# Attention scores of one stage: keys laid out block-diagonally, two heads per matmul

## The chip, the cores and the metric

The kernel runs on one core of a Trainium2 chip. The core has a matmul engine (TensorE, PE in the rows), a vector engine (VectorE, DVE), a scalar engine (ScalarE, ACT), GpSimd (POOL) and SyncE (SP), which starts the transfers here. Each engine works through its own instructions in order and waits on semaphores for the others. The metric is the device time of one execution in microseconds (us). The kernel before takes 2413.01 us, the median of three runs (2412.48 to 2414.86).

## The reference

The program is four layers, each an attention followed by a feed-forward part, over 64 sequences of 64 tokens of width 128. The change lies in the second of the eight parts, the feed-forward of layer 0, which is itself an attention whose values come from experts:

```python
def _L0_ffn_ref(x, w_q, w_k, w_gate, value_experts, output_experts):
    # HEADS, DIM_HEAD, EXPERTS = 8, 64, 8; x is the layer-normed stream
    q = (x @ w_q).reshape(b, n, HEADS, DIM_HEAD).transpose(0, 2, 1, 3)
    k = (x @ w_k).reshape(b, n, HEADS, DIM_HEAD).transpose(0, 2, 1, 3)
    gates = jax.nn.sigmoid((x @ w_gate).reshape(b, n, HEADS, EXPERTS).transpose(0, 2, 1, 3))
    gm = jax.nn.one_hot(jnp.argmax(gates, axis=-1), EXPERTS, dtype=x.dtype) * gates
    values = jnp.einsum('bhne,ehdk,bnd->bhnk', gm, value_experts, x)
    sim = jnp.einsum('bhid,bhjd->bhij', q * DIM_HEAD ** (-0.5), k)
    sim = jnp.where(causal_mask, jnp.finfo(sim.dtype).min, sim)
    out = jnp.einsum('bhij,bhjk->bhik', jax.nn.softmax(sim, axis=-1), values)
    out = jnp.einsum('bhne,ehkd,bhnk->bhnd', gm, output_experts, out)
    return out.sum(axis=1)
```

## The kernel before

`l0_ffn` runs over 8 groups (g) of 4 tiles (t); a tile is 128 tokens, two sequences (b) of 64. The 8 heads go in 4 pairs (c), of two heads (a) each. The q and k projections put the two heads of a pair on partitions 0 to 63 and 64 to 127, so that qT and kT are [128, 4 pairs, 512 tokens].

Each engine has its program written out by hand, and the order of work is the order of the calls. For each tile PE does the 8 expert values (`expert_values`, L971), one matmul per expert, and DVE picks by a mask after each (`pick`, L1201 and L1206). Between them PE transposes the outputs of the tile before the last (`turn_out`, L1018) and the probabilities of the tile before (`turn_probs`, L997). Then come `scores` (L981 the causal mask, L987 the products) and `values` (L1010). DVE does the row maximum (L1215) and the subtraction (L1218) of the scores; ACT the exponential (L1111); DVE the sums, their reciprocals and a product with the gate (L1224, L1226, L1229), and later the scaling of the outputs (L1237). POOL multiplies the picked values by the gate (`gate_values`, L917).

At the end of a group PE also projects q and k of the next (`project`, L962), and ACT copies each projection out of PSUM (`copy_q`, L1094; `copy_k`, L1100), between its copies of the turned outputs (L1124), and then does the gate's tanh (L1104), for which DVE waits (L1191). Then PE runs 32 matmuls of the output experts (L1027), each for a product that DVE makes (L1247). A semaphore in `scores` makes PE wait until the scores of the tile before are subtracted (`sub_done`). POOL begins the stage with three fills or casts (`setup_done`), for which all wait, and then copies the first input (L905).

A kernel line that is one matmul of fp32 numbers shows as two MATMUL records: the 16 products of a tile are 32 records. The third stage, `l1_xattn`, has the layout that the change brings: L1470 is its mask, L1476 its score products, L1499 its value products, L1724 the row maximum, L1606 its key copies.

Of the kernel before, what the change touches and what calls it, by code (L numbers as in the profile page):

```python
# [15 lines left out]
ALU = mybir.AluOpType  # L16
ACT = mybir.ActivationFunctionType
AX = mybir.AxisListType

P = 128  # L20
SEQ = 64
# [3 lines left out]
G = 4  # L25
GROUPS = TILES // G
GT = G * P
# [51 lines left out]
def count(n):  # L79

    return n + 1


def after(eng, sem, value):

    if not isinstance(value, int) or value > 0:
        eng.wait_ge(sem, count(value))
# [18 lines left out]
class Core:  # L106
# [29 lines left out]
    def sb(self, ctx, name, shape, dt=F32):  # L136
        return ctx.enter_context(self.nc.sbuf_tensor(name, shape, dt))

    def ps(self, ctx, name, shape=(P, 512), dt=F32):
        return ctx.enter_context(self.nc.psum_tensor(name, list(shape), dt))  # L140

    def sem(self, name):
        return self.ctx.enter_context(self.nc.semaphore(name))
# [46 lines left out]
def bcast(ap, axis, n):  # L190

    ap = ap.unsqueeze(axis)
    shape = list(ap.shape)
    shape[axis] = n
    return ap.broadcast_to(shape)
# [41 lines left out]
def norm_gpsimd(core, nc, pool, s, u, m=G, eps=1e-5):  # L237

    pool.wait_ge(s.mv, count(u * m + m))
    pool.sem_inc(s.may_invert, 1)  # L240
    nc.gpsimd.tensor_scalar(core.ve[:, 0:m], core.mv[:, 0:m, 1], eps, None, ALU.add).then_inc(s.eps, 1)  # L241
    pool.wait_ge(s.eps, count(u + 1))
    nc.gpsimd.tensor_tensor(core.rs[:, 0:m], core.ve[:, 0:m], core.half[:, 0:m], ALU.pow).then_inc(s.rstd, 1)
# [567 lines left out]
def l0_ffn(core, nc, d):  # L811
# [10 lines left out]
    H, HD, E = 8, 64, 8  # L822
    C = H // 2
# [5 lines left out]
    with ExitStack() as ctx:  # L829
        sb = lambda name, shape, dt=F32: core.sb(ctx, "l0f_" + name, shape, dt)  # L830
        ps = lambda name, shape=(P, 512), dt=F32: core.ps(ctx, "l0f_" + name, shape, dt)
        sem = core.counters(1)
        causal = sb("causal", [P, SEQ], BF16)
# [9 lines left out]
        oh_bf = sb("oh_bf", [P, G, P], BF16)  # L843
        ohT = sb("ohT", [P, GT], BF16)
        qT = sb("qT", [P, C, GT])
        kT = sb("kT", [P, C, GT])
        val = sb("val", [P, 2, H, HD])
        v2 = sb("v2", [P, 2, 2, C, 2, HD])
        diff = sb("diff", [P, H, SEQ])
        prob = sb("prob", [P, 2, H, SEQ])  # L850
        mx = sb("mx", [P, 2, H])
# [4 lines left out]
        z = sb("z", [P, Z, GT])  # L856
        yT = core.xn[:, 0, :, :].rearrange("p j d -> p (j d)")
        work = [ps(f"work{i}") for i in range(2)]
        score = ps("score", (P, 1024)).rearrange("p (a n) -> p a n", a=2)
        turn, po, acc, misc = ps("turn"), ps("po"), ps("acc"), ps("misc")  # L860
        value_banks = (work[0], work[1], acc)
        oh_turn = misc[:, 256:512].bitcast(BF16)
# [1 line left out]
        setup_done, xs_ready, lg_done, chain = sem("setup_done"), sem("xs_ready"), sem("lg_done"), sem("chain")  # L864
        top_ready, tanh_done, oh_ready, oh_turned, ohT_ready = (sem("top_ready"), sem("tanh_done"), sem("oh_ready"),
                                                                sem("oh_turned"), sem("ohT_ready"))
        qk_done, qk_copied = sem("qk_done"), sem("qk_copied")
        ve_done, pick_done, v2_ready = sem("ve_done"), sem("pick_done"), sem("v2_ready")
        score_done, sub_done, exp_done, tot_done = sem("score_done"), sem("sub_done"), sem("exp_done"), sem("tot_done")
# [5 lines left out]
        gated, may_pick, max_done, sum_done = sem("gated"), sem("may_pick"), sem("max_done"), sem("sum_done")  # L875

        with nc.Block() as block:
# [19 lines left out]
            @block.gpsimd  # L897
            def _(pool):
                nc.gpsimd.tensor_copy(causal[:, :], core.const("caus_n")).then_inc(setup_done, 1)
                nc.gpsimd.memset(oh_bf[:, :, :], 0.0).then_inc(setup_done, 1)  # L900
                nc.gpsimd.memset(v2[:, :, :, :, :, :], 0.0).then_inc(setup_done, 1)

                def stage(u):
                    after(pool, ve_done, u * G * E)
                    nc.gpsimd.tensor_copy(xs[:, :], core.xnT[:, bass.ds(u * GT, GT)]).then_inc(xs_ready, 1)  # L905

                gate = top[:, 2, :].rearrange("p (t h) -> p t h", t=G)

                def gate_values(g, t):
                    n = g * G + t  # L910
                    pool.wait_ge(pick_done, count((n + 1) * E))
                    after(pool, pv_done, n - 1)
                    for b in range(2):
                        for a in range(2):
                            r = slice(b * SEQ, (b + 1) * SEQ)
                            after(pool, v2_ready, n * 4 + 2 * b + a)
                            nc.gpsimd.tensor_tensor(  # L917
                                v2[a * SEQ:(a + 1) * SEQ, t % 2, b, :, a, :],
                                val[r, t % 2, :, :].rearrange("p (c a) k -> p c a k", a=2)[:, :, a, :],
                                bcast(gate[r, t, :].rearrange("p (c a) -> p c a", a=2)[:, :, a], 2, HD),  # L920
                                ALU.mult).then_inc(v2_ready, 1)
                    pool.wait_ge(v2_ready, count(n * 4 + 4))

                def group(g, more):
                    for t in range(1, G):
                        if t == G - 1 and more:
                            stage(g + 1)
                        gate_values(g, t)
                    if more:
                        gate_values(g + 1, 0)  # L930
                    norm_gpsimd(core, nc, pool, ns, g)

                stage(0)
                gate_values(0, 0)
                group(0, True)
                with pool.Fori(1, GROUPS - 1) as g:
                    group(g, True)
                group(GROUPS - 1, False)

            @block.tensor  # L940
            def _(pe):
                pe.wait_ge(core.w_loaded[1], 16)
                pe.wait_ge(setup_done, count(3))

                def logits(u):
                    pe.wait_ge(xs_ready, count(u + 1))
# [29 lines left out]
                            later()  # L976

                def scores(g, t):
                    after(pe, sub_done, g * G + t)
                    for a in range(2):  # L980
                        nc.tensor.matmul(score[:, a, 0:C * SEQ], core.ident_bf[:, :], bcast(causal[:, :], 1, C),  # L981
                                         start=True, stop=False, skip_group_check=True)
                    for c in range(C):
                        for b in range(2):
                            for a in range(2):
                                r, tok = slice(a * HD, (a + 1) * HD), slice(t * P + b * SEQ, t * P + (b + 1) * SEQ)
                                ins = nc.tensor.matmul(score[b * SEQ:(b + 1) * SEQ, a, c * SEQ:(c + 1) * SEQ],  # L987
                                                       qT[r, c, tok], kT[r, c, tok], start=False, stop=True,
                                                       skip_group_check=True)
                    ins.then_inc(score_done, 1)  # L990

                def turn_probs(g, t):
# [92 lines left out]

            @block.scalar
            def _(act):
                act.wait_ge(setup_done, count(3))

                def copy_q(u, chunks):  # L1090
                    after(act, score_done, u * G)
# [4 lines left out]
                def copy_k(u, chunks):  # L1096
                    after(act, score_done, u * G)
                    for c in chunks:
                        act.wait_ge(qk_done, count(u * 2 * C + C + c + 1))
                        nc.scalar.activation(kT[:, c, :], work[c % 2][:, :], ACT.Copy).then_inc(qk_copied, 1)  # L1100

                def gate_tanh(u):
                    act.wait_ge(top_ready, count(u + 1))
# [66 lines left out]

            @block.vector
            def _(dve):
                dve.wait_ge(setup_done, count(3))
                prio = bcast(core.const("prio"), 1, G * H)
                gate = top[:, 2, :].rearrange("p (t h) -> p t h", t=G)

# [32 lines left out]

                def softmax(g, t):  # L1210
                    n = g * G + t
                    s = score[:, :, 0:C * SEQ].rearrange("p a (c k) -> p a c k", c=C)
                    by_pair = mx[:, t % 2, :].rearrange("p (c a) -> p a c", a=2)
                    dve.wait_ge(score_done, count(n + 1))
                    nc.vector.tensor_reduce(by_pair, s, AX.X, ALU.max).then_inc(max_done, 1)  # L1215
                    dve.wait_ge(max_done, count(n + 1))
                    after(dve, exp_done, n)
                    nc.vector.tensor_tensor(diff[:, :, :].rearrange("p (c a) k -> p a c k", a=2), s, bcast(by_pair, 3, SEQ),  # L1218
                                            ALU.subtract).then_inc(sub_done, 1)

                def totals(g, t):
                    n = g * G + t
# [1841 lines left out]
def program(nc, d, out):  # L3064
    with ExitStack() as ctx:
        core = Core(nc, ctx)
        l0_xattn(core, nc, d)
        l0_ffn(core, nc, d)
        late_weights(core, nc, d)
        l1_xattn(core, nc, d)  # L3070
        with ExitStack() as late:
            km = core.sb(late, "keys_by_head", [P, G, 2, 16, SEQ])
            l1_ffn(core, nc, km)
            narrow_attention(core, nc, d, 4, True, km)
            l2_ffn(core, nc, d)
            narrow_attention(core, nc, d, 6, False, km)
        l3_ffn(core, nc, out)
# [112 lines left out]
```

## Time and profile before

| what | value |
|---|---|
| median of the runs | 2413.01 us |
| the profiled execution's own time | 2412.48 us |
| its span, first to last instruction | 2410.3 us |
| PE busy in the span | 2090.6 us, 87% |
| DVE busy | 1657.9 us, 69% |
| ACT busy | 862.7 us, 36% |
| POOL busy | 610.8 us, 25% |
| mean granted TensorE clock | 0.922 of full |

The stage of the change runs from about 149 us to 850 us of the span. Busy shares are over the whole program; what decides is which engine waits for which in this stage. In the rows of a timeline the bracket at the end is the idle time of the engine just before the row, and what ended it; a row without a bracket followed its predecessor.

### The profile page before, as it was taken

To read this page: it belongs to the slowest core of one execution; us is meant where nothing else is said; L and a number is where in the kernel's file an instruction comes from. 1 tells how busy PE (TensorE), PEld (TensorE's weight loads), DVE (VectorE), ACT (ScalarE), POOL (GpSimd) and SP (SyncE) were. 2 spreads that over 40 slices of the span, in tenths; PEclk is the share of its full clock that TensorE was granted. 3 is DMA by queue.
4 is the path that set the end of the run, shared out by engine and by line. 5 is a ranking of instruction groups with operands and counts; after the bars stand their busy time and mean duration, and the time that the engine had idled before them with its cause. 6 is when DMAs were issued, how large, how long until landed. Compare 5 with 4: busy or idle time off the path is not lost. (4 is left out here: it accounts for less than half of the span.)

```text
span 2410.3 us, 39647 instructions
## 1 busy us (share of the span) xinstructions
PE 2090.6 (87%) x12969; PEld 1154.9 (48%) x12971; DVE 1657.9 (69%) x3378; ACT 862.7 (36%) x1527; POOL 610.8 (25%) x832
## 2 busy tenths in 40 slices
PE   4769899899999879999999899689979999769965
PEld 2634444444444446666666544245544444335531
DVE  4767676777777756777777589667746667446668
ACT  4511201201211046666666554223332222223435
POOL 4641110111111044455555333222200000111201
PEclk8579999999999989999999999789979999989976
DMA  4403212230320421111111000000003433210001
GB/s 103 148 1 71 55 44 45 53 71 17 71 53 18 105 82 35 34 33 35 31 34 35 24 1 1 1 12 12 11 20 93 109 82 82 63 21 12 12 3 35
DMA packets 131760, 106.43 MB, mean 44 GB/s; under 512 B 95400, under 2 KB 113704, under 8 KB 127152
## 3 DMA queue, kind: packets, MB, share of 16 engines
q1 hardware_dynamic: 131632, 104.84, 17.7%
q8 instruction: 66, 1.08, 0.2%
q14 instruction: 62, 0.51, 0.1%
HBM read 80.85 MB, written 2.97 MB: 35 GB/s over the span
## 5 line engine op out<-in xcount | busy, mean ns | idle before, releaser
L1027 PE MATMUL l0f_acc<-l0f_z,w_all 128*128 128x512 f32 x512 | 230.1, 612 | 21.3 <-DVE l0f_z L1247 21.3
L917 POOL TENSOR_TENSOR l0f_v<-l0f_val,l0f_top 64x256 f32<-64x256 f32 x128 | 78.3, 612 | 506.5 <-DVE l0f_val L1206 498.9
L971 PE MATMUL l0f_work<-w_all,l0f_xs 128*128 128x512 f32 x384 | 187.6, 612 | 11.5 <-DVE l0f_val L1201 10.8
L1027 PEld LDWEIGHTS l0f_acc<-l0f_z,w_all 128*128 128x128 f32 x512 | 99.6, 196 | 151.4 <-issue 125.4
L241 POOL TENSOR_SCALAR var_eps<-mean_var 128x4 f32<-128x4 f32 (+1 forms) x64 | 14.5, 227 | 544.7 <-DVE mean_var L225 542.8
L2285 PE MATMUL a_score<-keys_by_head,a_qT 128*64 128x512 f32 x512 | 144.3, 646 | 9.0 <-DMA keys_by_head<-w_all 9.0
L1206 DVE COPY_PREDICATED l0f_val<-l0f_oh,l0f_work 128x512 f32<-128x512 int32 x160 | 116.8, 730 | 46.8 <-PE l0f_work L971 28.8
L2777 DVE TENSOR_TENSOR l2f_hu<-l2f_act_g,l2f_pu 128x512 f32<-128x512 f32 x104 | 71.1, 684 | 69.2 <-ACT l2f_act_g L2703 68.0
L2652 PE MATMUL l2f_acc<-l2f_hid,w_all 128*128 128x512 f32 x208 | 107.4, 598 | 9.8 <-DVE l2f_hid L2783 9.8
L2703 ACT ACTIVATE l2f_act_g<-l2f_pg 128x512 f32<-128x512 f32 x104 | 61.5, 594 | 149.5 <-PE l2f_pu L2644 137.6
L1707 DVE TENSOR_REDUCE l1x_ms_k<-l1x_sq_k 128x8 f32<-128x512 f32 x64 | 43.9, 685 | 102.9 <-ACT l1x_sq_k L1593 102.9
L971 PEld LDWEIGHTS l0f_work<-w_all,l0f_xs 128*128 128x128 f32 x384 | 68.9, 192 | 86.5 <-issue 54.1
L2643 PE MATMUL l2f_pg<-xnT_all,w_all 128*128 128x512 f32 x208 | 109.0, 606 | 0.0
L2644 PE MATMUL l2f_pu<-xnT_all,w_all 128*128 128x512 f32 x208 | 108.0, 601 | 0.0
L1247 DVE TENSOR_TENSOR l0f_z<-l0f_oT,l0f_first_mask 128x512 f32<-128x512 f32 x128 | 87.3, 692 | 27.6 <-PE l0f_acc L1027 24.1
L1386 POOL TENSOR_TENSOR l1x_rs_q<-l1x_ms_q,minus_half 128x8 f32<-128x8 f32 x64 | 104.8, 1637 | 5.7 <-POOL l1x_ms_q L1382 0.8
L1395 POOL TENSOR_TENSOR l1x_rs_k<-l1x_ms_k,minus_half 128x8 f32<-128x8 f32 x64 | 104.7, 1636 | 5.4 <-POOL l1x_ms_k L1391 0.2
L1606 ACT ACTIVATE l1x_kb<-l1x_turn,cols 64x512 f32<-64x512 f32 x128 | 87.3, 682 | 51.3 <-PE l1x_turn L1459 50.5
L1247 DVE TENSOR_TENSOR l0f_z<-l0f_oT,w_all 128x512 f32<-128x512 f32 x128 | 88.7, 693 | 21.1 <-PE l0f_acc L1027 20.8
L2466 DVE TENSOR_REDUCE a_mx<-a_score 128x16 f32<-128x1024 f32 x64 | 78.0, 1219 | 32.9 <-PE a_score L2285 32.7
L2407 ACT ACTIVATE a_oT<-a_po 128x128 f32<-128x128 f32 x64 | 17.7, 277 | 210.4 <-PE a_po L2315 210.4
L1157 ACT ACTIVATE xn<-l0f_acc 128x512 f32<-128x512 f32 x8 | 4.8, 597 | 245.7 <-PE l0f_acc L1027 245.7
(362 smaller groups left out, 4804.5 us busy)
## 6 DMA issues: line engine op xcount, KB each, us to landing
l0f_first_mask<-onehots SPq DMA_DIRECT2D x32, 512.0 KB, 5.7
w_all<-onehots SPq DMA_DIRECT2D x32, 512.0 KB, 11.9
l1x_v<-l1x_vr SPq DMA_DIRECT2D x256, 64.0 KB, 2.1
w_all<-combination SPq DMA_DIRECT2D x40, 256.0 KB, 5.3
w_all<-in_weights SPq DMA_DIRECT2D x1, 4640.0 KB, 17.3
l0x_m_b<-running_max SPq DMA_DIRECT2D x16, 256.0 KB, 4.5
keys_by_head<-w_all SPq DMA_DIRECT2D x256, 8.0 KB
keys_by_head<-ctxT_all SPq DMA_DIRECT2D x256, 8.0 KB
```

The lines of the kernel that those rows point to most:

```text
L917: nc.gpsimd.tensor_tensor(v2[a * SEQ:(a + 1) * SEQ, t % 2, b, :, a, :], val[r, t % 2, :, :].rearrange("p (c a) k -> p c a k", a=2)[:, :, a ...
L971: nc.tensor.matmul(value_banks[e % 3][:, :], xs[:, t * P:(t + 1) * P], ve[:, e, :], start=True, stop=True).then_inc(ve_done, 1)
L1027: nc.tensor.matmul(acc[:, :], oe[:, n % E, n // E, :], z[:, n % Z, :], start=(n == 0), stop=(n == C * E - 1)).then_inc(acc_done, 1)
L1206: nc.vector.copy_predicated(val[:, t % 2, :, :], m_e, w3).then_inc(pick_done, 1)
L1247: nc.vector.tensor_tensor(z[:, n % Z, :], oT[:, n // E, :], masks[n // E][:, n % E, :], ALU.mult)\
L1386: nc.gpsimd.tensor_tensor(rs_q[:, :], ms_q[:, 1, :], core.half[:, 0:HU], ALU.pow).then_inc(rs_q_done, 1)
L1395: nc.gpsimd.tensor_tensor(rs_k[:, :], ms_k[:, 1, :], core.half[:, 0:HU], ALU.pow).then_inc(rs_k_done, 1)
L1606: ins = nc.scalar.activation(kb[r, :, :, a, :], turn1[r, :].rearrange("p (c b k) -> p c b k", c=C, b=2), ACT.Copy, scale=core.col("l1_kw") ...
L2285: ins = nc.tensor.matmul(s[b * SEQ:(b + 1) * SEQ, cols], qT[:, half, t * P + b * SEQ:t * P + (b + 1) * SEQ], km[:, t, b, bank * C:(bank + ...
L2643: nc.tensor.matmul(pg[n % 3][:, :], wg[:, c * P:(c + 1) * P], x_of(g), start=True, stop=True)
L2644: nc.tensor.matmul(pu[n % 3][:, :], wu[:, c * P:(c + 1) * P], x_of(g), start=True, stop=True)\
L2652: nc.tensor.matmul(acc[:, :], wd[:, c * P:(c + 1) * P], hid[:, n % 3, :], start=(c == 0), stop=(c == CH - 1)).then_inc(acc_done, 1)
```

## The change

The two-bank score tensor becomes two tensors of one bank, taken in turn by even and odd tiles, and `scores` waits for the subtraction of the tile before the last. The transposed keys are kept as `kb`, zero outside the blocks: for a tile, a sequence and a pair it is [128 partitions, 2 heads x 64 keys], with head 0's keys on the first 64 partitions and head 1's on the last 64. One matmul with all 128 partitions then gives the scores of both heads. It takes 16 KB per partition, where kT took 8. POOL fills it with zeros once, ahead of v2; ACT copies each key projection in two halves of 64 partitions. The maximum and the subtraction read the heads in their order.

```diff
-        kT = sb("kT", [P, C, GT])
+        kb = sb("kb", [P, G, 2, C, 2, SEQ])
-        score = ps("score", (P, 1024)).rearrange("p (a n) -> p a n", a=2)
+        score = [ps(f"score{i}") for i in range(2)]
...
+                nc.gpsimd.memset(kb[:, :, :, :, :, :], 0.0).then_inc(setup_done, 1)
                 nc.gpsimd.memset(v2[:, :, :, :, :, :], 0.0).then_inc(setup_done, 1)
...
-                pe.wait_ge(setup_done, count(3))
+                pe.wait_ge(setup_done, count(4))
...
                 def scores(g, t):
-                    after(pe, sub_done, g * G + t)
-                    for a in range(2):
-                        nc.tensor.matmul(score[:, a, 0:C * SEQ], core.ident_bf[:, :], bcast(causal[:, :], 1, C),
-                                         start=True, stop=False, skip_group_check=True)
+                    after(pe, sub_done, g * G + t - 1)
+                    nc.tensor.matmul(score[t % 2][:, :], core.ident_bf[:, :], bcast(causal[:, :], 1, H),
+                                     start=True, stop=False, skip_group_check=True)
                     for c in range(C):
                         for b in range(2):
-                            for a in range(2):
-                                r, tok = slice(a * HD, (a + 1) * HD), slice(t * P + b * SEQ, t * P + (b + 1) * SEQ)
-                                ins = nc.tensor.matmul(score[b * SEQ:(b + 1) * SEQ, a, c * SEQ:(c + 1) * SEQ],
-                                                       qT[r, c, tok], kT[r, c, tok], start=False, stop=True,
-                                                       skip_group_check=True)
+                            ins = nc.tensor.matmul(score[t % 2][b * SEQ:(b + 1) * SEQ, c * P:(c + 1) * P],
+                                                   qT[:, c, t * P + b * SEQ:t * P + (b + 1) * SEQ],
+                                                   kb[:, t, b, c, :, :].rearrange("p a k -> p (a k)"),
+                                                   start=False, stop=True, skip_group_check=True)
...
                         act.wait_ge(qk_done, count(u * 2 * C + C + c + 1))
-                        nc.scalar.activation(kT[:, c, :], work[c % 2][:, :], ACT.Copy).then_inc(qk_copied, 1)
+                        for a in range(2):
+                            r = slice(a * HD, (a + 1) * HD)
+                            ins = nc.scalar.activation(kb[r, :, :, c, a, :],
+                                                       work[c % 2][r, :].rearrange("p (t b k) -> p t b k", t=G, b=2),
+                                                       ACT.Copy)
+                        ins.then_inc(qk_copied, 1)
...
-                    nc.vector.tensor_reduce(by_pair, s, AX.X, ALU.max).then_inc(max_done, 1)
+                    nc.vector.tensor_reduce(mx[:, t % 2, :], s, AX.X, ALU.max).then_inc(max_done, 1)
```

PE in the first group, around the scores of the second tile, before (the number in front of a shape's first x is the output's partitions):

```order
L971 MATMUL l0f_work<-w_all,l0f_xs 128x512 x2
L981 MATMUL l0f_score<-l0f_causal,ident_bf 128x256 x2
L987 MATMUL l0f_score<-l0f_kT,l0f_qT 64x64 x16
L1010 MATMUL l0f_po<-l0f_v,l0f_probT 64x128 x8
L1038 MATMUL l0f_misc<-ident_bf,l0f_oh_bf 128x128 x4
```

and the same place after the change:

```order
L972 MATMUL l0f_work<-w_all,l0f_xs 128x512 x2
L981 MATMUL l0f_score<-l0f_causal,ident_bf 128x512
L985 MATMUL l0f_score<-l0f_kb,l0f_qT 64x128 x8
L1009 MATMUL l0f_po<-l0f_v,l0f_probT 64x128 x8
L1037 MATMUL l0f_misc<-ident_bf,l0f_oh_bf 128x128 x4
```

Nothing changes place; one mask matmul stands for two, and 8 products of 128 columns for 16 of 64.

ACT at the end of the first group, from the last two q copies to the copy after the output experts, before:

```order
L1094 ACTIVATE l0f_qT<-l0f_work 128x512 x2
L1118 ACTIVATE l0f_probT<-l0f_turn 128x512
L1100 ACTIVATE l0f_kT<-l0f_work 128x512 x3
L1124 ACTIVATE l0f_oT<-l0f_turn 128x4x128
L1100 ACTIVATE l0f_kT<-l0f_work 128x512
L1104 ACTIVATE l0f_top<-l0f_top 128x32
L1157 ACTIVATE xn<-l0f_acc 128x512
```

and after:

```order
L1093 ACTIVATE l0f_qT<-l0f_work 128x512 x2
L1122 ACTIVATE l0f_probT<-l0f_turn 128x512
L1101 ACTIVATE l0f_kb<-l0f_work 64x8x64 x6
L1128 ACTIVATE l0f_oT<-l0f_turn 128x4x128
L1101 ACTIVATE l0f_kb<-l0f_work 64x8x64 x2
L1108 ACTIVATE l0f_top<-l0f_top 128x32
L1161 ACTIVATE xn<-l0f_acc 128x512
```

Each key copy is two instructions now; they stand ahead of the copy of the turned outputs and of the tanh, as the single ones did.

## Rows read from the trace of the kernel before

**Rows 1.** timeline, second group, second tile: start, duration, engine, line, wait.
```profile
261.36 0.38 PE L981 MATMUL l0f_score<-l0f_causal,ident_bf 128*128 128x256 bf16 x2
...
261.67 0.69 PE L987 MATMUL l0f_score<-l0f_kT,l0f_qT 64*64 64x64 f32 x32
...
262.30 1.09 PE L1010 MATMUL l0f_po<-l0f_v,l0f_probT 128*64 128x128 f32 x16
262.44 0.69 DVE L1215 TENSOR_REDUCE l0f_mx<-l0f_score 128x8 f32<-128x512 f32 x1
262.78 2.68 POOL L917 TENSOR_TENSOR l0f_v<-l0f_val,l0f_top 64x256 f32<-64x256 f32 x4 [6.00 <-DVE l0f_val L1206]
...
264.81 0.17 DVE L1229 TENSOR_TENSOR l0f_tot<-l0f_tot,l0f_top 128x8 f32<-128x8 f32 x1
...
268.40 0.66 PE L1018 MATMUL l0f_turn<-consts,l0f_og 128*128 128x128 f32 x4 [2.04 <-DVE l0f_og L1237]
```

**Rows 2.** timeline, third stage, whose scores have the other layout.
```profile
1001.69 0.38 PE L1470 MATMUL l1x_score<-l1x_mask,ident_bf 128*128 x1
...
1002.00 1.09 PE L1476 MATMUL l1x_score<-l1x_kb,l1x_qT 128*64 128x128 f32 x16
...
1002.93 1.04 PE L1499 MATMUL l1x_po<-l1x_v,l1x_probT 128*64 128x128 f32 x16
...
1003.14 0.69 DVE L1724 TENSOR_REDUCE l1x_mx<-l1x_score 128x8 f32<-128x512 f32 x1 [0.21 <-PE l1x_score L1476]
```

**Rows 3.** timeline, line L1229 in later and earlier tiles.
```profile
182.14 0.57 DVE L1229 TENSOR_TENSOR l0f_tot<-l0f_tot,l0f_top 128x8 f32<-128x8 f32 x1
...
276.56 2.68 POOL L917 TENSOR_TENSOR l0f_v<-l0f_val,l0f_top 64x256 f32<-64x256 f32 x4 [11.11 <-DVE l0f_val L1206]
...
278.66 0.60 DVE L1229 TENSOR_TENSOR l0f_tot<-l0f_tot,l0f_top 128x8 f32<-128x8 f32 x1
...
805.78 0.56 DVE L1229 TENSOR_TENSOR l0f_tot<-l0f_tot,l0f_top 128x8 f32<-128x8 f32 x1
```

**Rows 4.** timeline, start of the stage.
```profile
149.95 1.80 POOL L901 MEMSET l0f_v<- 128x2048 f32 x1
...
152.45 1.94 PE L950 MATMUL l0f_misc<-w_all,l0f_xs 128*128 128x64 f32 x8 [4.05 <-POOL l0f_xs L905]
...
160.05 0.60 ACT L1100 ACTIVATE l0f_kT<-l0f_work 128x512 f32<-128x512 f32 x1 [0.26 <-PE l0f_work L962]
...
163.47 1.98 PE L971 MATMUL l0f_work<-w_all,l0f_xs 128*128 128x512 f32 x4 [0.69 <-ACT l0f_kT L1100]
```

**Rows 5.** lines by form, a larger fill: shape, count, busy us, mean ns.
```profile
L1859 POOL MEMSET keys_by_head<- 128x8192 f32 x1 | 6.9, 6923 | 0.1
```

**Rows 6.** timeline, third stage, two copies of 64 partitions.
```profile
999.57 1.38 ACT L1606 ACTIVATE l1x_kb<-l1x_turn,cols 64x512 f32<-64x512 f32 x2
```

**Rows 7.** timeline, end of the second group.
```profile
289.49 1.94 PE L962 MATMUL l0f_work<-xnT_all,w_all 128*128 x4
...
291.26 0.60 PE L1018 MATMUL l0f_turn<-consts,l0f_og 128*128 128x128 f32 x4
...
296.86 0.69 DVE L1237 TENSOR_TENSOR l0f_og<-l0f_po,l0f_tot 128x512 f32<-128x512 f32 x1 [4.74 <-PE l0f_po L1010]
...
297.85 0.60 ACT L1100 ACTIVATE l0f_kT<-l0f_work 128x512 f32<-128x512 f32 x1 [1.48 <-PE l0f_work L962]
...
298.35 0.59 ACT L1124 ACTIVATE l0f_oT<-l0f_turn 128x512 f32<-128x512 f32 x1
...
299.66 0.22 ACT L1104 ACTIVATE l0f_top<-l0f_top 128x32 f32<-128x32 f32 x1
...
300.84 0.17 DVE L1191 TENSOR_SCALAR l0f_top<-l0f_top 128x32 f32<-128x32 f32 x1
```

**Rows 8.** windows: us, busy by engine (records), granted clock, DMA share, GB/s.
```profile
268.40:272.70 4.30, 4.30 (x12) 2.37 (x13) 1.71 (x3) 0.60 (x1) 0.00 (x0) 0.60 1.06 236
356.00:360.30 4.30, 4.29 (x16) 2.41 (x17) 2.50 (x4) 1.19 (x2) 0.00 (x0) 1.00 1.01 211
```

More of the change, by code:

```diff
@@ L1087, in _ @@
             def _(act):
-                act.wait_ge(setup_done, count(3))
+                act.wait_ge(setup_done, count(4))
                 def copy_q(u, chunks):
@@ L1172, in _ @@
             def _(dve):
-                dve.wait_ge(setup_done, count(3))
+                dve.wait_ge(setup_done, count(4))
                 prio = bcast(core.const("prio"), 1, G * H)
@@ L1211, in softmax @@
                     n = g * G + t
-                    s = score[:, :, 0:C * SEQ].rearrange("p a (c k) -> p a c k", c=C)
-                    by_pair = mx[:, t % 2, :].rearrange("p (c a) -> p a c", a=2)
+                    s = score[t % 2][:, :].rearrange("p (h k) -> p h k", h=H)
                     dve.wait_ge(score_done, count(n + 1))
-                    nc.vector.tensor_reduce(by_pair, s, AX.X, ALU.max).then_inc(max_done, 1)
+                    nc.vector.tensor_reduce(mx[:, t % 2, :], s, AX.X, ALU.max).then_inc(max_done, 1)
                     dve.wait_ge(max_done, count(n + 1))
                     after(dve, exp_done, n)
-                    nc.vector.tensor_tensor(diff[:, :, :].rearrange("p (c a) k -> p a c k", a=2), s, bcast(by_pair, 3, SEQ),
-                                            ALU.subtract).then_inc(sub_done, 1)
+                    nc.vector.tensor_tensor(diff[:, :, :], s, bcast(mx[:, t % 2, :], 2, SEQ), ALU.subtract)\
+                        .then_inc(sub_done, 1)
                 def totals(g, t):
```

## The prediction

> **What bounds the kernel now.** I read the timeline of the stage first, then its waits, then the granted clock. In a tile DVE and PE take turns. [rows 1] show it for the second tile of the second group: PE's score products start at 261.67 and end at 262.36, DVE takes the row maximum (L1215) 0.08 us later, and with no wait in the row. From there DVE leads: maximum, subtraction, sums, gate product L1229, two picks, scaled outputs, and PE has idled 2.04 us when L1018 starts on those outputs at 268.40. Then PE leads to the next scores. So the end of the scores and DVE's chain behind it are on the path, and PE's time between scores and L1018 is not. At the end of a group PE leads alone: [rows 7] have L962 from 289.49 and L1018 at 291.26 without a wait, and DVE idles 4.74 us for PE's values before L1237. DVE then has its expert picking, ended by L1191, which waits for ACT's tanh (L1104).
>
> **The score products.** Before: 32 records of 64 rows by 64 columns, from 261.67 to the start of L1010 at 262.30, 0.63 us. After: 16 records of 128 rows and 128 columns. That form stands in the third stage [rows 2]: from L1476 at 1002.00 to L1499 at 1002.93 is 0.93 us, and from L1476 to DVE's maximum, which waits for it, is 1.14 us. In [rows 1] this last distance is 262.44 - 261.67 = 0.77. So the halves of the array that worked side by side on the two heads now work on one product whose other half is zeros: PE pays 0.93 - 0.63 = 0.30 us a tile, DVE starts 1.14 - 0.77 = 0.37 us later. The mask costs nothing either way: L981 to L987 is 0.31 us [rows 1], L1470 to L1476 0.31 us [rows 2].
>
> The Trainium skill (TensorEngine Tiling (Array Packing), Theoretical Speedup) gives up to 2x for a contraction of 64 or less, so taking the row tiles away should double the products. The rows of the two forms, 0.63 and 0.93 us, show a factor of 1.5. By the page the products would take 1.26 us, 0.63 more, and my term for the seven group ends below would be 4.4 us in place of 2.1; I go by the rows.
>
> The wait on the subtraction gains nothing. On DVE the subtraction of a tile stands ahead of all 8 picks of the next, and PE's scores stand behind the expert values that those picks release; no row of L981 has a wait on DVE [rows 1]. The second score bank removes a wait that is never last.
>
> What the delay of a tile becomes depends on its place:
> - *First tile of a group* (8): in seven, DVE first adds the outputs to x and takes statistics, and PE is ahead. 0. The very first tile has no such cover: at most 0.37, I take 0.1.
> - *Second tile, groups 2 to 7* (6): L1229 starts at 264.81 in 0.17 us, just ahead of the last of POOL's four products, which end at 262.78 + 2.68 = 265.46 [rows 1]. In 12 other places L1229 takes 0.52 to 0.60 us, of which [rows 3] have the first, one between and the last; the one at 278.66 ends at 279.26, and POOL's four products end at 276.56 + 2.68 = 279.24. So L1229 waits for a POOL product that has begun. Moved by 0.37 to 265.18 it falls into the last one and ends at 265.46 or so in place of 264.98: 0.48 x 6 = 2.9 us.
> - *Third tile of all, second tile of groups 1 and 8, fourth of group 8* (11): there L1229 already waits for POOL. Ready 0.37 later (279.03 in [rows 3]) it still ends with POOL at 279.24, since POOL's start hangs on the last pick and not on the scores. 0; without that shelter 11 x 0.37 = 4.1.
> - *Fourth tile, groups 1 to 7* (7): PE leads without a gap, so its own 0.30 counts: 2.1 us. No cover here.
>
> **The fill.** A POOL fill of 2048 elements takes 1.80 us [rows 4], one of 8192 takes 6.92 [rows 5]: 0.833 ns an element, so 4096 take 1.80 + 2048 x 0.000833 = 3.5 us. It stands ahead of the copy L905, and PE's first matmul L950 has idled 4.05 us for that copy [rows 4], DVE and ACT wait for PE. Nothing else runs there: +3.5, once; I see no way to hide it.
>
> **The key copies.** One copy of 128 partitions is 0.60 us [rows 4]. Two of 64 partitions in the third stage take 1.38 us for the pair [rows 6], one behind the other; they carry a scale for each partition, ours none. I take 0.61 apiece; the ends are 0.50 (the distance from a key copy at 297.85 to the next copy at 298.35 [rows 7]) and 0.69.
> - *Start of the stage*: 8 half copies from 160.05 end at 164.93, and the expert values L971, which started at 163.47 after a wait for the last key copy [rows 4], start at 164.98: +1.5 (ends 0.5 and 2.2).
> - *Group ends* [rows 7]: the third key copy starts at 297.85, its halves end at 299.07, L1124 follows, the fourth key's halves run from 299.57 to 300.79 and the tanh ends at 301.01. L1191 had started at 300.84: it starts 0.2 later, seven times, +1.4. Before, the tanh was done at 299.88, so the first 0.96 us of the longer copies are hidden behind DVE's expert picking. With 0.50 apiece all is hidden (0), with 0.69 it is 0.54 x 7 = 3.8.
> - Reading one bank instead of two changes nothing: the maximum takes 0.69 us in both forms [rows 1, 2].
>
> **Sum.** 3.5 + 1.5 + 0.1 + 2.9 + 2.1 + 1.4 = 11.5 us. The profiled execution took 2412.48 us by its own time, 0.5 under the median of the runs, so 2424.0 us. All lower ends together (no cost in the second tiles) give 3.5 + 0.5 + 2.1 = 6.1; all upper ends 3.5 + 2.2 + 0.4 + 2.9 + 4.1 + 2.1 + 3.8 = 19.0.
>
> **The clock** is the part that I can't place. [rows 8] have two stretches of the same work in two groups: at a mean granted clock of 0.60 PE gets through 12 records, at 1.00 through 16. The first is mostly at 1.2 GHz, and loses 4.30 x (1 - 0.60) = 1.7 us. Such stretches stand eight times in the stage, in four of the groups' third tiles and at four of their ends, and otherwise equal groups differ by them. A group that gets 1 us longer meets them elsewhere: I allow three more or fewer, 5 us.
>
> **Rivals.**
> - *No shelter at L1229*: what makes L1229 long could be something else than POOL's products, and the 11 delays come through: 2424.0 + 4.1 = 2428.1. For it: at 264.81 it runs in 0.17 amid them. Against: the ends match to 0.02 us [rows 3]. The Trainium skill (SBUF — State Buffer, SBUF: two separate sides) has VectorE with two SBUF inputs and GpSimd exclude each other for a whole instruction, which would give the shelter; these rows agree.
> - *Dear half copies*: 0.69 apiece adds 0.7 at the start and 2.4 at the group ends: 2427.1. For it the pair in [rows 6], against it the missing scale.
> - *Cheap products*: if a record costs the same 0.02 us (0.63 / 32) whatever its shape, 16 take 0.31 and PE gains 0.3 a tile: 3.5 + 1.5 + 1.4 - 2.1 = 4.3, 2416.8 us, which is no measurable change. Against it stands L1476 in [rows 2].
> - *The clock pays it back*, on the other side: if low stretches go, each gives 1.7 us. Four fewer leave 4.7 us, below what can be told from none; seven fewer cancel all, and all eight give 2410.4 us. For it: half of such places have none now. Against: PE's idle before L1018 stays about as long, so their cause stays.
>
> **Chances.** The forecast 0.67, no shelter 0.10, dear copies 0.08, cheap products 0.06, the clock 0.09. The first three are slower by over 0.2% (4.8 us, about what a measurement of this kernel can tell from no change): 0.85. Cheap products and two thirds of the clock case are within: 0.12; faster 0.03. The forecast's own range is 2419 to 2429, with the rivals 2416.5 to 2431.
>
> **What the new profile would show.** A 128x4096 fill of 3.5 us and PE's first matmul of the stage 3.5 us later; 16 score records and 0.93 us from the first to the values; DVE's maximum now with a wait on PE's scores; L1229 long in the second tiles too, with POOL's end; PE's idle before the turned outputs about as before; half copies of 0.60, and L1191 waiting for the tanh. The forecast is wrong if the maximum starts as early as before, if the halves overlap, or if the number of stretches below full clock moves by more than three.

## The result and the profile after

The changed kernel takes 2437.46 us in the median (2432.83 to 2439.78, six runs) against 2413.94; the ratio is 1.009, with a 95% interval of 1.0074 to 1.0107. Slower was forecast, with 2424.0 us and a range to 2431. The forecast size was half of the measured one, and the time lies outside the range.

The profiled execution took 2432.44 us, 20.0 more than that of before. Its timeline in the second group, second tile, against [rows 1]:

```profile
269.51 1.09 PE L985 MATMUL l0f_score<-l0f_kb,l0f_qT 128*64 128x128 f32 x16
270.43 1.04 PE L1009 MATMUL l0f_po<-l0f_v,l0f_probT 128*64 128x128 f32 x16
...
270.65 0.69 DVE L1218 TENSOR_REDUCE l0f_mx<-l0f_score 128x8 f32<-128x512 f32 x1 [0.30 <-PE l0f_score L985]
...
273.02 0.30 DVE L1232 TENSOR_TENSOR l0f_tot<-l0f_tot,l0f_top 128x8 f32<-128x8 f32 x1
...
276.54 0.66 PE L1017 MATMUL l0f_turn<-consts,l0f_og 128*128 128x128 f32 x4 [2.11 <-DVE l0f_og L1240]
277.04 3.58 PE L972 MATMUL l0f_work<-w_all,l0f_xs 128*128 128x512 f32 x4
...
287.20 0.23 DVE L1232 TENSOR_TENSOR l0f_tot<-l0f_tot,l0f_top 128x8 f32<-128x8 f32 x1
```

From the first score product to the first value product it is 0.92 us. The row maximum starts 1.14 us after the first score product, and now with a wait for PE. L1232 (L1229 before) takes 0.30 us for 0.17 and ends at 273.32, with the last of POOL's products (273.30). The last row is the same line in the third tile: it starts 0.20 us before the end of POOL's products (287.40), where it started 0.58 before it ([rows 3]), and ends with them as before. All this was forecast. The start of the stage, against [rows 4]:

```profile
149.87 3.51 POOL L901 MEMSET l0f_kb<- 128x4096 f32 x1
...
155.83 1.94 PE L951 MATMUL l0f_misc<-w_all,l0f_xs 128*128 128x64 f32 x8 [7.51 <-POOL l0f_xs L906]
...
163.92 4.86 ACT L1101 ACTIVATE l0f_kb<-l0f_work 64x512 f32<-64x512 f32 x8 [0.26 <-PE l0f_work L963]
...
168.83 1.98 PE L972 MATMUL l0f_work<-w_all,l0f_xs 128*128 128x512 f32 x4 [1.31 <-ACT l0f_kb L1101]
```

The fill takes 3.51 us, and 8 half copies take 4.86, 0.61 apiece. L972 starts 5.36 us later than before. 3.38 of it stand already at L951 and come from the fill. From the first key copy to L972 it is 4.91 us (168.83 - 163.92) for 3.42 before, so the half copies add 1.49, as forecast (1.5). The 0.49 us that are left arise ahead of the first key copy, between the first two q copies. Before, and after:

```profile
157.38 0.60 ACT L1094 ACTIVATE l0f_qT<-l0f_work 128x512 f32<-128x512 f32 x1 [0.48 <-PE l0f_work L962]
```

```profile
161.25 0.60 ACT L1093 ACTIVATE l0f_qT<-l0f_work 128x512 f32<-128x512 f32 x1 [0.98 <-PE l0f_work L963]
```

ACT waits 0.50 us longer for PE there: from the first q copy to the second the mean granted clock is 0.58, where it was 0.85. The end of the second group, against [rows 7]:

```profile
309.50 0.23 ACT L1108 ACTIVATE l0f_top<-l0f_top 128x32 f32<-128x32 f32 x1
309.76 0.18 DVE L1195 TENSOR_SCALAR l0f_top<-l0f_top 128x32 f32<-128x32 f32 x1
...
310.91 5.40 PE L1026 MATMUL l0f_acc<-l0f_z,w_all 128*128 128x512 f32 x8 [3.07 <-DVE l0f_z L1250]
```

The tanh is now what DVE waits for (L1195 starts 0.03 us after its end; before it was 0.96), and PE idles 3.07 us ahead of the output experts, where it had 2.86. What differs from the forecast is in the granted clock (columns as in [rows 8]). After the third tile's idle time in the third group, where [rows 8] has 1.00 (at 356.00), it is now 0.60:

```profile
365.26:369.56 4.30, 4.30 (x12) 2.13 (x13) 1.40 (x3) 0.60 (x1) 0.00 (x0) 0.60 1.04 217
```

And the output experts at the end of the first group, before and after:

```profile
216.47:221.97 5.50, 5.50 (x13) 2.55 (x14) 4.53 (x8) 0.00 (x0) 0.00 (x0) 1.00 0.00 0
```

```profile
222.77:228.27 5.50, 5.50 (x10) 2.46 (x11) 3.39 (x6) 0.00 (x0) 0.00 (x0) 0.72 0.00 0
```

So both places now have a stretch that is mostly at the lower level, 1.2 GHz; I call it a low stretch. Low stretches can be counted from the distance of one row maximum to the next: 12.25 us before and 12.57 after from the second tile to the third at full clock, 1.7 more with a low stretch; likewise from the fourth tile to the next group. Before has 8 such places, 4 in third tiles (groups 2, 5, 6 and 7) and 4 at group ends (2, 3, 4 and 7). After has 12: third tiles of groups 2, 3, 4, 6 and 7, and all 7 group ends. The record of the granted clock has the same 8 and 12.

At the first mask matmul of the next stage the changed kernel is 20.7 us behind (889.71 against 869.03). Of this, 5.5 us arise up to the first row maximum, 13.3 from the first maximum to the last, with 4 x 1.7 = 6.8 of clock in them, and 1.9 after the last maximum, where the forecast had nothing. The stretch from the last maximum to the next stage, before and after:

```profile
803.50:869.03 65.53, 46.56 (x136) 22.33 (x136) 36.67 (x64) 8.02 (x14) 10.77 (x14) 0.82 0.31 105
```

```profile
822.29:889.71 67.42, 48.69 (x137) 23.06 (x133) 36.28 (x63) 8.03 (x14) 10.54 (x14) 0.77 0.30 103
```

### The profile page after: what moved, and what is told of

Its sections match the earlier page's. It is cut to its first block and busy times, and to the rows that moved or that the text cites. A ratio compares the mean times of both kernels' runs of the same rounds, so it can differ in the third digit from the quotient of the medians.

```text
span 2430.6 us, 38588 instructions
## 1 busy us (share of the span) xinstructions
PE 2107.6 (87%) x12427; PEld 1162.5 (48%) x12427; DVE 1658.2 (68%) x3378; ACT 882.9 (36%) x1559; POOL 614.3 (25%) x833
## 5 line engine op out<-in xcount | busy, mean ns | idle before, releaser
L1026 PE MATMUL l0f_acc<-l0f_z,w_all 128*128 128x512 f32 x512 | 236.5, 625 | 22.8 <-DVE l0f_z L1250 22.8
L972 PE MATMUL l0f_work<-w_all,l0f_xs 128*128 128x512 f32 x384 | 190.2, 619 | 9.5 <-DVE l0f_val L1205 8.2
L972 PEld LDWEIGHTS l0f_work<-w_all,l0f_xs 128*128 128x128 f32 x384 | 69.5, 194 | 86.0 <-issue 56.8
## 6 DMA issues: line engine op xcount, KB each, us to landing
w_all<-onehots SPq DMA_DIRECT2D x32, 512.0 KB, 11.1
```

Of the source, the lines that this page charges most:

```text
L972: nc.tensor.matmul(value_banks[e % 3][:, :], xs[:, t * P:(t + 1) * P], ve[:, e, :], start=True, stop=True).then_inc(ve_done, 1)
L1026: nc.tensor.matmul(acc[:, :], oe[:, n % E, n // E, :], z[:, n % Z, :], start=(n == 0), stop=(n == C * E - 1)).then_inc(acc_done, 1)
```

## Experiments

Beside each of these kernels the kernel before was measured anew; its medians lie between 2413.0 and 2415.3 us. A difference between two changed kernels that were not measured side by side is uncertain by as much. Where an experiment has "coupling" or "idle-length" theory in its expectation, these are my two guesses on where the low stretches come from: that one brings on the next, or that the length of PE's idle time decides.

**Does the clock hold the missing time? PE's idle time filled.** `causal` is the mask; `turn` and `po` are PSUM banks that are free at these places, and the next matmuls overwrite them.

```diff
+                def fill(bank, m):
+                    for _ in range(m):
+                        nc.tensor.matmul(bank[:, :], core.ident_bf[:, :], bcast(causal[:, :], 1, 8),
+                                         start=True, stop=True)
...
-                        expert_values(g, t + 1, (lambda: turn_out(g, t - 1)) if t else None, lambda: turn_probs(g, t))
+                        expert_values(g, t + 1, (lambda: (fill(turn, 6 if t == 1 else 0), turn_out(g, t - 1))) if t else None,
+                                      lambda: turn_probs(g, t))
...
+                    fill(po, 9)
                     output_experts(g)
```

> The kernel before, with idle PE time of this stage filled: 6 mask matmuls into the turn bank ahead of the turned outputs of the third tile (there PE idled 2.04 us), 9 into the po bank ahead of the output experts (2.85 us idle), both banks free there. Clock theory (the extra 8 us of the change are four more stretches at the lower clock, which follow PE's idle times): no granted clock below full in the groups, eight stretches of 1.7 us gone, 13 us faster than before, about 2400 us. Rival (the low stretches come from something else than PE's idle time, or the fill delays what follows): same as before or slower, 2413 to 2425.

> The changed kernel with the same fill. Clock theory: its 12 stretches go too, so that it stands 11.5 to 12.5 us above the filled kernel before (2412), and not 20 to 23. Rival (the change costs 20 us by its own work, in places that I have not seen): it stays 20 us or more above the filled kernel before.

Measured: the filled kernel before takes 2402.3 us, ratio 0.9949 (0.9936 to 0.9962) to before. The filled changed kernel takes 2413.8, ratio 0.9997 (0.9989 to 1.0006) to before. In both every step from maximum to maximum is the short one, so no low stretch is left between the first maximum and the last. These are the fill in the third tile of the filled kernel before, and the clock of the stretch that follows it:

```profile
266.36 1.46 PE L1036 MATMUL l0f_turn<-l0f_causal,ident_bf 128*128 128x512 bf16 x6
268.57 0.66 PE L1018 MATMUL l0f_turn<-consts,l0f_og 128*128 128x128 f32 x4 [0.75 <-DVE l0f_og L1244]
```

```profile
268.57:272.87 4.30, 4.30 (x16) 2.41 (x17) 2.50 (x4) 1.19 (x2) 0.00 (x0) 1.00 1.07 240
```

PE idles 0.75 us there instead of 2.04, and does 16 records in the time in which [rows 8] has 12 at the lower clock. The change costs 2413.8 - 2402.3 = 11.5 us between these two (give or take 4, from the two intervals), as the sum had it; the fill gives 12.6 us back before and 2437.5 - 2413.8 = 23.7 after. The rival (20 us of own work) is out.

The granted clocks of all these runs say the same. The time that a run lacks to full clock, its span times (1 - mean granted clock), averages 188 us in the kernel before and 176 filled, 202 us in the changed kernel and 179 filled: 12 and 23 us less by the fill. And all 65 low stretches of the 14 profiled kernels between the first maximum and the last begin at an idle time of PE of 2.03 to 3.07 us, from 1.0 us before its end to 1.4 us after it.

**The parts, with the clock as it is.** The first has, in place of the one fill of kb, two fills of 2048 elements:

```diff
+                nc.gpsimd.memset(qT[:, :, :], 0.0)
+                nc.gpsimd.memset(kT[:, :, :], 0.0).then_inc(setup_done, 1)
...
-                pe.wait_ge(setup_done, count(3))
+                pe.wait_ge(setup_done, count(4))
...
```

> The kernel before with two fills of 2048 elements more on POOL at the start of the stage, which all wait for, as the changed kernel's one of 4096. Sum of the prediction: +3.5 us, profile span 2413.8. Clock theory: +3.5 us plus a whole number of stretches of 1.7 us more or fewer, since only the time at which the groups meet the clock moves; all groups' own steps otherwise as before. Rival (the fill costs nothing, hidden): 0.

2417.9 us against 2414.9, ratio 1.0015 (1.0005 to 1.0025): 3.0 us (3.5 forecast), and PE's first matmul of the stage starts at 155.87, as in the changed kernel (155.83). There are 8 low places as before, at other groups (third tiles of groups 2, 3, 7 and 8; before 2, 5, 6 and 7). A shift alone moves them and doesn't add any. PE's idle times are as long as before (2.04 and 2.85 us), so the moment at which an idle time comes has a say in whether it is followed by the lower clock.

The scores alone are the changed kernel without its fill and its half copies. It leaves out the zeros: a product here adds both heads of a pair, so the output is another, but the shapes are those of the change.

```diff
-                                                   kb[:, t, b, c, :, :].rearrange("p a k -> p (a k)"),
+                                                   kT[:, c, t * P:(t + 1) * P],
...
```

> The changed scores alone: 8 products of all 128 partitions and 128 columns, one mask matmul, a bank in turn, but kT copied as before, no fill of zeros; the products add both heads of a pair, so the output is not the reference's. Prediction's terms as the new profile corrects them: 0.3 in the second tiles of six groups and 0.3 at seven group ends, 4 us, and 0 from the key copies; 4 us more than before but for stretches of the clock. Rival (the four more low stretches come from the scores themselves, through a PE period 0.3 us longer): 4 + 6.7 = 11 us. Rival (products no dearer): 0 or less.

> The changed scores alone (both heads of a pair are added, so the output is not the reference's), with PE's idle time filled by mask matmuls at the two places. No low stretch, so the scores' own price: 0.3 us in six second tiles, 0.3 at seven group ends and 0.3 in the first tile, 4.2 us above the filled kernel before (2402.3): 2406.5. Rival (the scores' 10.6 us are their own work): 2413.

2425.6 us without the filled idle time, ratio 1.0041 (1.0028 to 1.0054), 10.6 more than before; 2408.2 with it, 5.9 above the filled kernel before, where I had expected 4.2; its profile shows 5.1 us from the first maximum to the last. The profile of the unfilled one has 10 low places, 5 in third tiles and 5 at group ends.

The half copies alone:

```diff
-                        nc.scalar.activation(kT[:, c, :], work[c % 2][:, :], ACT.Copy).then_inc(qk_copied, 1)
+                        for a in range(2):
+                            r = slice(a * HD, (a + 1) * HD)
+                            ins = nc.scalar.activation(kT[r, c, :], work[c % 2][r, :], ACT.Copy)
+                        ins.then_inc(qk_copied, 1)
```

> The kernel before, with each key projection copied by two instructions of 64 partitions and nothing else changed. Mechanism: +1.5 to 1.9 us at the start, 0.2 us at seven group ends, together 3.1. It also lengthens PE's idle time ahead of the output experts by those 0.2 us, 2.85 to 3.07. Idle-length theory of the low stretches: all seven group ends are then low (four before), and +3.1 + 5 = 8 us. Rival (only the time at which groups meet the clock matters): about 8 stretches in all as before, 3 us with either sign of 1.7.

> The halved key copies alone on the filled kernel before. Own price 1.9 + 7 x 0.2 = 3.3 us above 2402.3: 2405.6. With the fill of zeros at 3.5 and the scores at 4.2 this makes the 11.5 us between the two filled kernels. Rival (terms overlap or hide each other): the three add up to other than 11.5.

2419.7 us unfilled, ratio 1.0030 (1.0018 to 1.0041), 5.5 more than before, between the 8 and the 3 of the two theories; 2405.2 filled, 2.9 above the filled kernel before. Unfilled there are 10 low places, 6 of them at the 7 group ends (four before), where PE idles 3.06 us; the idle-length theory had said 7. Filled, the parts are 3.0 + 5.9 + 2.9 = 11.8 us (the 3.0 from the unfilled pair), the whole is 11.5, each with an uncertainty of a few us. The traces are sharper: from the first maximum to the last the scores add 5.1 us, the half copies 1.45, and the whole change 6.8. The parts don't hide one another.

**The wait on the subtraction**, put back in the filled changed kernel:

```diff
-                    after(pe, sub_done, g * G + t - 1)
+                    after(pe, sub_done, g * G + t)
```

> The changed kernel, filled, with the wait for the subtraction of the tile before put back. Prediction: this wait is never the last, 0 us against the filled changed kernel (2413.8), and the same steps from tile to tile. Rival (the second score bank lets PE run ahead): slower than it by up to 32 x 0.3 us = 10 us.

2414.5 us against 2413.8, and the steps between the maxima are the same to 0.02 us. The second score bank gains nothing, as forecast.

**What brings the four stretches more?** The changed kernel with other numbers of mask matmuls at the two places, then the kernel before: 1 and 1, 0 and 9, 6 and 0; before: 0 and 9.

> The changed kernel with a single mask matmul (0.22 us) in each of the two idle times of PE, so that these are about as long as in the kernel before (1.9 and 2.85 us against 2.04 and 2.85; 2.11 and 3.07 in the changed kernel). Idle-length theory: low stretches at group ends fall from seven to four or so and in the third tiles from five to four or fewer; 4 or more stretches gone, 7 us or more below the changed kernel (2437.5): 2430 or lower. Rival (the period of a group, about 88.2 us at the lower clock, decides, not the length of the idle times): still 12 or so, 2436 to 2438.

> The changed kernel with only the idle time ahead of the output experts filled (9 mask matmuls). Both theories: the seven stretches at the group ends go, 7 x 1.7 = 12 us; those in the third tiles stay at five: 2425.5. Rival (a low stretch that is kept away at one place comes at the other, since the clock looks at PE over time): third tiles all low, 2429.

> The changed kernel with only the third tiles' idle time filled (6 mask matmuls). Coupling theory by the group end (its idle time of 3.07 us is the longer one and sets the others off): the seven stretches at the ends stay and the five in the third tiles go, 12 less 5: 2437.5 - 8.5 = 2429. Rival (either fill breaks the chain): 2414 to 2418.

> The kernel before with only the idle time ahead of the output experts filled (9 mask matmuls). In the changed kernel this alone gave as much as both fills (2413.8). Coupling theory (a low stretch at a group end brings the next ones, also in the third tiles): about as fast as the kernel before with both fills, 2402 to 2404. Rival (each idle time has its own stretches): the four at the ends go, 6.8 us, the four in the third tiles stay: 2407.

| kernel | median, us | ratio to before (95%) | low places: third tiles | at group ends |
|---|---|---|---|---|
| before, none | 2413.9 | 1 | 4 | 4 |
| after, none | 2437.5 | 1.0090 (1.0074 to 1.0107) | 5 | 7 |
| after, 1 and 1 | 2423.7 | 1.0037 (1.0023 to 1.0051) | 0 | 5, two of 3 us |
| after, 6 and 0 | 2427.0 | 1.0050 (1.0036 to 1.0063) | 0 | 5, two of 3 us |
| after, 0 and 9 | 2413.8 | 1.0005 (0.9996 to 1.0014) | 1 | 0 |
| before, 0 and 9 | 2409.5 | 0.9974 (0.9964 to 0.9985) | 6 | 0 |

Where a step is 3 us longer instead of 1.7, the granted clock has one low stretch of double length.

One mask matmul at each place takes 13.8 us off the changed kernel (12.8 by the two ratios), as the idle-length theory expected (2430 or lower). The idle time ahead of the output experts then is what it was before:

```profile
308.77 0.38 PE L1035 MATMUL l0f_po<-l0f_causal,ident_bf 128*128 128x512 bf16 x1
312.00 18.27 PE L1026 MATMUL l0f_acc<-l0f_z,w_all 128*128 128x512 f32 x38 [2.85 <-DVE l0f_z L1257]
```

So the extra low time is not work, and the length of the idle times has a say: in the third tiles 1.89 us of it brings no low stretch. With the third tiles filled alone the time is 2427.0 us, near the 2429 expected, and not the 2414 to 2418 of the rival; five group ends stay low, two of them for double length, where seven had been expected.

But it isn't length alone. With the ends filled, the third tiles are low six times of eight in the kernel before, at 2.04 us idle, and once in the changed kernel, at 2.11. The row maxima of second and third tile in the third group, of the kernel before with filled ends, and of the changed kernel with filled ends:

```profile
348.42 0.69 DVE L1222 TENSOR_REDUCE l0f_mx<-l0f_score 128x8 f32<-128x512 f32 x1
...
362.36 0.69 DVE L1222 TENSOR_REDUCE l0f_mx<-l0f_score 128x8 f32<-128x512 f32 x1
```

```profile
355.67 0.69 DVE L1225 TENSOR_REDUCE l0f_mx<-l0f_score 128x8 f32<-128x512 f32 x1 [0.30 <-PE l0f_score L985]
...
368.23 0.69 DVE L1225 TENSOR_REDUCE l0f_mx<-l0f_score 128x8 f32<-128x512 f32 x1 [0.36 <-PE l0f_score L985]
```

13.94 us there, 12.56 here. So when an idle time comes also matters. The changed kernel with filled ends took 2413.8 us, where 2425.5 and, by the rival, 2429 had been expected: four of its five low third tiles went with the ends. I made the coupling theory from this result, and the next run didn't bear it out: the kernel before with filled ends took 2409.5 us, where the theory had 2402 to 2404 and the rival 2407, and it has two more low third tiles than unfilled. Which idle times bring the lower clock is not settled by these runs; they show that the length and the moment both count, and that filling both places keeps it away.

The fastest version here is the kernel before with both fills, 2402.3 us.

## Why the prediction was wrong

The sum of the change's own work came out, in part by luck, and the clock term did not. The table has the steps of the filled kernels, where no low stretch is in the way (us, from one row maximum to the next, groups 4 to 7). In the forecast the maximum comes 0.37 us later in the second to fourth tiles, and not in the first; so these 0.37 count in the first step and drop out in the last.

| step | before | changed | forecast of the difference |
|---|---|---|---|
| first to second tile | 8.06 | 8.43 | 0.37 |
| second to third | 12.26 | 12.57 | 0.48 |
| third to fourth | 11.31 | 11.34 | 0 |
| fourth to next group | 52.34 | 52.47 | 0.30 + 0.20 - 0.37 = 0.13 |

- *Products*: 0.92 us as forecast. The mask was free, one bank instead of two too, the wait was never last. Cheap products are out.
- *Shelter at L1229*: right, third to fourth tile 0.03. In the third tile of the second group the line began 0.38 us later against POOL's products and took 0.23 us in place of 0.60. The rival without shelter is out. In the second tiles the cost was 0.31 and not 0.48: before, the normalisation after L1229 began 0.15 us late, and now 0.02, its four instructions taking 1.12 instead of 1.19 us; I had left this out. Over six groups it is 1.9 us for 2.9.
- *First group*: its first to second tile takes 8.09 before and 8.74 after, 0.3 more than in later groups, where I had 0.1 for the first tile.
- *Fill and half copies*: 3.4 and 1.49 for 3.5 and 1.5. Half copies cost 0.61 apiece, so that rival is out too. In every profiled kernel it is 4.9 us from the first key copy to the expert values with half copies and 3.3 to 3.4 without. The other 0.49 us at the start are clock: PE's projections ran longer at the lower level, after PE had idled 7.51 us for the longer fill and not 4.05.
- *The total*: in the two filled traces the next stage begins 12.7 us later (868.47 against 855.76), 4.8 up to the first maximum (5.1 in the sum), 6.8 from there to the last (6.4), and 1.1 after it, for which the sum had nothing. Too much in the second tiles and too little in the first group and at the end nearly cancel, so that 11.5 on both sides is in part luck.
- *The clock*, the step that failed: "I allow three more or fewer, 5 us". I had put the clock at nothing in the sum. The profiled execution has four more low stretches, 6.8 us, and the medians say 23.7 - 12.6 = 11.1 us more low time than before. I had taken the count as a throw of dice around eight, since PE's idle time before L1018 stays about as long, and looked only at this one place. At the group ends the term that I had sized myself (L1191 0.2 later) makes PE's idle time longer by the same 0.2, from 2.85 to 3.07 us, and all seven are followed by a low stretch in place of four. Half copies alone gave two low places more, the scores alone two more. All my rivals with the clock were on the faster side. With the term at its measured 11 us the forecast would have been 2435.

The profiled execution is 3.5 us nearer to before than the medians, and this too is clock: it lacks 194 us to full clock, and the six other runs 202 on average. What stays open is what decides for one idle time of 2 to 3 us and against the next, and why the half copies and the scores, each alone, bring low stretches at the places where they do.

## What to carry to other kernels

Where PE idles 2 to 3 us again and again, a change is to be priced twice: its own steps, and what it does to the clock after each of these idle times, which here was as large (some 11 us each). To measure the first alone, fill the idle times with matmuls into a free bank in both kernels, and look in the trace whether the granted clock now stays up; this gave 11.5 us where the plain pair gave 23.5. Two products in one with zeros between save no PE time when the small ones already ran side by side.

## What the runs showed of the hardware

- A granted clock that falls to half after idle times of 2.04 and 2.85 us in a PE that is busy nine tenths of the stage (in 4 of 8 third tiles and at 4 of 7 group ends, 1.7 us each), and 15 mask matmuls a group, some 3.6 us of PE work (1.46 + 2.11), that make the kernel 12.6 us faster.
- ACT copies of 64 partitions cost as much as of 128: 0.61 against 0.60 us.
- A POOL fill of fp32 zeros goes at 0.83 ns an element: 1.80, 3.51 and 6.92 us for 2048, 4096 and 8192.
- The 16 products of 64x64 of a tile take 0.63 us, and the 8 of 128x64 with the same useful work 0.92, a factor of 1.5.
